# Preparation, fill and end of a patch-attention and DCT kernel laid out anew, with the first turn behind tile ten

## The reference, cut to what matters

```python
def _L0_conv_ref(x, W1, b1, a1, W2, b2, a2, Wa, ba, aa, Wd, bd):
    embed_w = prelu(conv1x1(x, Wa, ba), aa)
    match_in = prelu(conv1x1(x, W1, b1), a1)
    raw_w = extract_patches(embed_w, 6, 2)
    ref = x.reshape(B, C, H // 2, 2, W // 2, 2).mean(axis=(3, 5))
    ref = prelu(conv1x1(ref, W2, b2), a2)
    w = extract_patches(ref, 3, 1)
    wn = (w / norm(w)).reshape(B, -1, C // 2 * 9)
    xp = extract_patches(match_in, 3, 1).reshape(B, -1, C // 2 * 9)
    yi = softmax(einsum('blc,bqc->blq', wn, xp) * 10, axis=1)
    yd = conv_stride_2(transposed_conv(yi, raw_w), Wd) + bd
    return yd / 6

x = x + _L0_conv_ref(_gn(x), ...)
x = x + dct2(_gn(x))
```

## Time and profile before

| | us |
|---|---|
| median of 3 runs | 232.2 |
| lowest and highest | 231.97 and 234.13 |
| the profiled execution's own time | 232.2 |
| its span from first to last instruction | 230.4 |
| PE busy | 182.9 (79%) |
| DVE busy | 142.3 (62%) |
| ACT busy | 118.1 (51%) |
| POOL busy | 122.4 (53%) |

### The profile page before, as it was taken

One profiled execution on the slowest core, in us unless ns is written; L12 is line 12 of the kernel. 1 busy time (PEld: TensorE's weight loads), 2 busy tenths in 40 slices (PEclk: granted clock), 3 DMA queues, 4 the chain that ended last, 5 costly groups with the idle time before them and its releaser, 6 DMA issues.

```text
span 230.4 us, 3498 instructions
## 1 busy us (share of the span) xinstructions
PE 182.9 (79%) x1112; PEld 147.9 (64%) x1112; DVE 142.3 (62%) x293; ACT 118.1 (51%) x209; POOL 122.4 (53%) x107
## 2 busy tenths in 40 slices
PE   1496606963797589396999999999998999698993
PEld 0444506942666478185888878987876776577790
DVE  5669815663576767867566666556778379577101
ACT  4875612657373467545575695565564356133020
POOL 8362101006478489488686599999999940000000
PEclk9996555899679659979999999999999999997687
DMA  5270076666140000243542511440064000004402
GB/s 155 46 129 10 9 138 102 104 116 181 44 77 0 4 0 1 34 81 68 114 126 82 123 32 30 80 81 4 4 127 125 3 3 1 0 0 83 75 3 51
DMA packets 16872, 14.09 MB, mean 61 GB/s; under 512 B 9974, under 2 KB 14646, under 8 KB 16726
## 3 DMA queue, kind: packets, MB, share of 16 engines
q1 hardware_dynamic: 15174, 12.83, 27.7%
q10 hardware_dynamic: 1680, 1.04, 1.6%
HBM read 2.14 MB, written 1.18 MB: 14 GB/s over the span
## 4 chain that ended last, share of the span: by engine, by line
PE 50%; DVE 20%; ACT 9%; POOL 8%; issue 7%; ACTq 3%; DMA 1%; DVEq 0%; SPq 0%; POOLq 0%
PE yt L915 12%; PE ps L873 11%; PE zt L899 9%; POOL nt L692 4%; DVE negm L1392 4%; ACT nt L1105 3%; ACTq L365 3%; PE zt L935 2%; DVE mimg L1338 2%; DVE mhi L1334 2%; PE ps L899 2%; PE yt L950 2%; PE zt L873 2%; ACT slanted L1067 2%; PE pm L943 2%
## 5 line engine op out<-in xcount | busy, mean ns | idle before, releaser
L692 POOL TENSOR_TENSOR nt<-nt 128x599 f32<-128x599 f32 (+1 forms) x51 | 69.2, 1357 | 31.7 <-ACT nt L1113 24.0
L915 PE MATMUL yt<-yf,kf 125*128 125x384 f32 (+1 forms) x120 | 49.6, 497 | 4.8 <-DVE yf L1409 4.7
L899 PEld LDWEIGHTS zt<-ident,nt 128*125 128x125 f32 (+1 forms) x300 | 40.2, 181 | 12.7 <-issue 2.5
L899 PE MATMUL zt<-ident,nt 128*125 128x128 f32 (+1 forms) x300 | 42.4, 279 | 0.1
L1113 ACT ACTIVATE nt<-nt,rps 128x599 f32<-128x599 f32 x36 | 28.7, 796 | 20.0 <-DVE rps L1399 19.9
L1105 ACT ACTIVATE nt<-ps,negm 128x576 f32<-128x576 f32 x31 | 22.9, 738 | 30.3 <-DVE negm L1392 30.3
L1392 DVE TENSOR_REDUCE negm<-ps 128x1 f32<-128x576 f32 x31 | 23.4, 754 | 16.3 <-PE ps L873 15.8
L873 PE MATMUL ps<-wh,vh 128*128 128x288 f32 x62 | 18.5, 383 | 17.6 <-DVE wr L1387 9.1
L873 PEld LDWEIGHTS ps<-wh,vh 128*128 128x128 f32 x62 | 10.7, 214 | 24.1 <-ACT nt L1105 13.8
L915 PEld LDWEIGHTS yt<-yf,kf 125*128 125x128 f32 (+1 forms) x120 | 18.8, 192 | 5.9 <-DVE yf L1409 5.1
L1409 DVE COPY yf<-zt 125x384 f32<-125x384 f32 (+1 forms) x28 | 19.4, 691 | 4.2 <-issue 3.0
...
...
## 6 DMA issues: line engine op xcount, KB each, us to landing
...
vh<-mimg SPq DMA_DIRECT2D x24, 72.0 KB, 2.5
vl<-mimg SPq DMA_DIRECT2D x24, 72.0 KB, 2.5
...
```

The costliest lines, as they stand in the source:

```text
L692: pool.tensor_tensor(nt[:, dst, (to + 1) * KP + 1:(to + 1) * KP + 1 + n], nt[:, one, (row1 + 1) * KP + 1:(row1 + 1) * KP + 1 + n], nt[:, o ...
L899: last = nc.tensor.matmul(turned(sums_bank(m), n, column), keys_at(tile, r + dr, n, shift), ident[:, :], start=at == 0, stop=at == len(wor ...
L915: nc.tensor.matmul(yt[:, k % 2, 0:CHUNK], kf[b][0:n, blk, :], yf[0:n, blk, :], start=blk == 0, stop=blk == KB - 1).then_inc(s_mb, 1)
```

## The change

It has five parts.

1. `BEGIN` and with it `FILL` go from 11 to 10. Turn 0 comes one tile earlier in the order, so that turn `k` starts in the order behind tile `3k + 11` in place of `3k + 12`; there are 46 steps in place of 47.
2. The queries of image 0 for chunks 1 to 5 are loaded together: 16 DMAs of 16 partitions by five chunks in place of 30 (and three of `vr` in place of 15). Tiles of chunks 1 to 5 wait for all of them (`arrived`). `vr` is now loaded after the keys on ACT, and the first tile waits for its four operands one by one.
3. The tables `BEFORE`, `SPREAD` and `BEHIND_PE` are new. The row jobs of image 1 come one in each step from step 2 on, and DVE does a row's maximum a step after ACT has made its `slanted`. The keys of image 1 come from step 15 on in place of 13; the copies after the eighth row are a job of their own.
4. The memset of the odd taps on POOL is replaced by two DMAs at the start. The bias addition on ACT covers one column of 48 pixels; the rest of the bias is added in `join_taps`, which is now two instructions for each part in place of one. The last sums (`last_sum`) start one step earlier.
5. In the list `behind` 5 `idle` matmuls stand in place of 14, and the last transforms of the two images are interleaved.

```diff
-BEGIN = 11
+BEGIN = 10
-    ("conv1", 0, (7,)), ("match", 0, (6, 7)), ("ninth", 0, (0, 1, 2)), ("inorm", 0, (0, 1)), ("keys", 0, (0, 1)),
-    ("mean", 1, (0,))]
+    ("conv1", 0, (7,)), ("match", 0, (6, 7)), ("inorm", 0, (0, 1)), ("mean", 1, (0,)), ("dup", 0, (0,)), ("keys", 0, (0, 1)),
+    ("after", 0, (0,)), ("ninth", 0, (0, 1)), ("weights", 1, (0,))]
...
-    ("conv1", 1, 8, 9, 3.5), ("match", 1, 8, 11, 3.5),
+    ("emb", 0, 2, 4, 1), ("conv1", 1, 8, 7, 3), ("match", 1, 8, 7, 3), ("squares", 1, 1, 9, 1), ("dup", 1, 1, 29, 1),
...
-    "act": {"conv2": 1, "conv1": 1, "emb": 1, "ek": 1, "zn": 1, "d1": 1, "match": 2},
+    "act": {"conv2": 1, "conv1": 1, "emb": 1, "ek": 1, "match": 7, "after": 5},
...
+    "dve": {"bias_2": 1, "bias_1": 1, "bias_a": 3, "conv2": 3, "conv1": 3, "emb": 3, "norm": 2, "inorm": 2, "keys": 2,
+            "match": 4, "dup": 4},
...
-    behind = stages(1, ("deviation", 1)) + stages(0, ("zn", 3), ("d1", 2))
-    behind += stages(1, ("x1n", 3)) + stages(0, ("d2", 2)) + [("idle", 1, 8)] + stages(1, ("zn", 3)) + [("idle", 1, 4)]
-    behind += stages(1, ("d1", 2)) + [("idle", 1, 2)] + stages(1, ("d2", 2))
+    behind = stages(1, ("deviation", 1)) + stages(0, ("zn", 3)) + [("idle", 1, 3)] + stages(0, ("d1", 2))
+    behind += stages(1, ("x1n", 3)) + [("d2", 0, 0)] + stages(1, ("zn", 3)) + [("d2", 0, 1), ("idle", 1, 2)]
+    behind += stages(1, ("d1", 2), ("d2", 2))
...
+        def arrived(eng, landed, g, images):
+
+            together = 16 * (3 if landed is s_vr else sum(n for _, n in SHIFTS))
+            if images == 1:
+                eng.wait_ge(landed[min(g, 1)], together if g else 48)
+            else:
+                eng.wait_ge(landed[g], (96, together + 48, 48)[min(g, 2)])
...
+                            for row in range(n):
+                                to = F(dst[3 * CR * k + row:3 * CR * k + row + 1, cols])
+                                wide = dst.shape[1]
+                                to = bass.AP(to.tensor, to.offset, [[n * wide, CR], [1, CHUNK * many]])
+                                sp.dma_start(to, bass.AP(src.tensor, at + BLOCK * row,
+                                                         [[pitch, CR], [BLOCK, many], [1, CHUNK]])).then_inc(done, 16)
...
+            sp.wait_ge(s_zero, 3)
+            for b in range(B):
+                odd = v2[2 * C * b + C:2 * C * (b + 1), :]
+                sp.dma_start(odd, F(vr[128 - C:128, :])).then_inc(s_apart[b], 16)
             ref_patches(0)
-            for t in range(NCH):
-                match_patches(0, t)
+            match_patches(0, 0)
+            match_patches(0, 1, NCH - 1)
...
-                pool.memset(v2[2 * C * b + C:2 * C * (b + 1), :], 0.0).then_inc(s_apart[b], 1)
...
-                part = x1_rows(b)
-                nc.scalar.activation(v2[part, :], v2[part, :], ACT.Identity, bias=bd6[part, 0:1]).then_inc(s_xres[b], 1)
+                first = strided(x1(b), 0, (W, H))
+                nc.scalar.activation(first, first, ACT.Identity, bias=bd6[x1_rows(b), 0:1]).then_inc(s_xres[b], 1)
...
-                nc.vector.tensor_tensor(even, even, odd, ALU.add).then_inc(s_x1[b], 1)
-                dve.wait_ge(s_x1[b], part + 1)
+                for n in range(2):
...
+                    nc.vector.scalar_tensor_tensor(out=even, in0=even, scalar=bd6[x1_rows(b), 0:1], in1=odd, op0=ALU.add,
+                                                   op1=ALU.add).then_inc(s_x1[b], 1)
+                    dve.wait_ge(s_x1[b], 2 * part + n + 1)
```

More of the change, by code:

```diff
@@ L360, in strided, with ninth @@
             return bass.AP(ap.tensor, ap.offset + start, [list(ap.ap[0])] + [list(d) for d in dims])
[L362 to L366 removed]
+        def ninth(eng, n, low, t, many=1):
+            src = F(mimg[64 + low:64 + low + CR, :])
+            at = src.offset + match_rows_at(1 + SHIFTS[2][0], t + 2, 0)
+            return eng.dma_start(F(vr[CR * n:CR * (n + 1), CHUNK * t:CHUNK * (t + many)]),
+                                 bass.AP(src.tensor, at, [[mimg.shape[1], CR], [BLOCK, many], [1, CHUNK]]))
+        def arrived(eng, landed, g, images):
[4 more added lines that the diff above has]
+                eng.wait_ge(landed[g], (96, together + 48, 48)[min(g, 2)])
         def patches_in(eng, images):
[L370 to L372 removed]
+            for g in range(NCH if images > 1 else 2):
+                for landed in (s_vh, s_vl, s_vr):
+                    arrived(eng, landed, g, images)
         def place_free(eng):
@@ L578, in _ @@
                     row_before(b)
-                sp.wait_ge(s_x1[b], 3)
+                sp.wait_ge(s_x1[b], 6)
                 sp.dma_start(x1_copy[b], x1(b)).then_inc(s_x1out[b], 16)
@@ L1026, in match_high @@
                         after(b, 1)
-                        after(b, 2)
                     return
@@ L1531, in _ @@
                     sums_copied(k, KB - 1)
+                if k == NG - 3 and j == 1:
+                    last_pair(NG - 2)
+                if k == NG - 3 and j == 2:
+                    last_sum(0)
+                if k == NG - 2 and j < 2:
+                    last_sum(j + 1)
+                if k == NG - 2 and j == 2:
+                    last_pair(NG - 1)
                 if k >= 1 and j == 2 and (k - 1) % NCH in (2, 4, 5):
@@ L1537, in _ @@
                         x1_statistics(b, 2 * part + 1)
-                if k == NG - 3 and j == 1:
-                    last_pair(NG - 2)
-                if k == NG - 2:
-                    last_sum(j)
-                if k == NG - 2 and j == 2:
-                    last_pair(NG - 1)
                 perform(gaps["dve"].get((s, 2), []), handlers)
```

81 lines of the change are left out of this document (39 added, 42 removed).

## The result

| | before | after | forecast |
|---|---|---|---|
| median | 232.69 (4 runs) | 242.96 (4 runs) | 220.0 |
| lowest and highest | 231.97, 234.13 | 242.68, 243.86 | range 211 to 228.5 |
| span of the profiled execution | 230.4 | 240.9 | 218.2 |

The changed kernel is slower: the ratio is 1.044, with a 95% interval of 1.039 to 1.050. The time lies far outside the range, on the other side.

The account below looks back on a forecast made before the run. PE was taken to bound the middle, POOL right behind it in later turns, and engines waiting in a ring the fill. 5.5 - 10.6 - 3.7 + 0.3 + 0 - 3.7 = -12.2 from 232.2 gives 220.0 us; range 211 to 228.5.

Parts of the forecast that it names:

- Start to tile 3: Start to tile 3's end: waiting for merged loads at 115 GB/s covers tile 0's 4 us gain; +5.5 us.
- Tile 3 to turn 0: Fill up to the tile ahead of turn 0: eight shorter tile steps in place of nine; -10.6 us.
- one more tile lies in it, 1.1 us of PE: Turn 4 to turn 9: the earlier start adds one tile there, costing 1.1 us of PE.
- Turns 0 to 3: Turns 0 to 3: fewer rows and long jobs, 47.0 us in place of 50.73; -3.7 us.
- slower rival: Fill: every high part and split waits for a whole POOL sum, turns win nothing; 235.0 us, chance 0.06.
- I price that wait at 1.2: Turns 2 and 3: keys come just ahead of the tile needing them; PE's wait costs 1.2 us.
- Turn 4 to turn 9: Turn 4 to turn 9: one more tile, against a bias addition and a memset that leave; +0.3 us.
- The seven pairs of `join_taps` cost some 0.1 us each beside other work: Tap joins on DVE: each of seven two-instruction pairs costs some 0.1 us beside other work.
- The end: Behind the last turn: image 1's transposes start at 214.0 in place of 217.74; -3.7 us.
- faster rival: Load up to tile 3: the 16 DMAs run at their issue pace, +5.5 becomes 0; 214.5 us, chance 0.20.

Follow-up runs that it names:

- chunk_loads: Changed kernel with SyncE's match-patch loads chunk by chunk again, with a wait for each chunk; 237.3 us, ratio 1.016 to the kernel before.
- before_keys_first: Kernel before with image 0's keys ahead of ScalarE's nine DMAs of the third part, nothing else; 230.9 us, ratio 0.991.
- begin_eleven: Changed kernel with the first turn eleven tile steps behind the first tile, as before the change; 244.2 us, ratio 1.039 to the kernel before.
- chunks_late_eleven: Changed kernel with loads, joins, bias, end list and image 1's late jobs as before, and the first turn eleven steps behind; 227.6 us, ratio 0.980.
- near_later: Changed kernel with two VectorE copies of image 1's doubled rows and columns moved behind the next maximum; 244.8 us, ratio 1.049 to the kernel before.
- keys_early: Changed kernel with image 1's scaled and split keys moved earlier in the table (36 and 39 for 42 and 45); 242.0 us, ratio 1.031.
- chunks_and_keys: Changed kernel with SyncE's loads chunk by chunk and image 1's keys two steps earlier; 233.9 us, ratio 0.998 to the kernel before.
- before_two_joins: Kernel before with only the changed tap joining: two instructions for a pair, and ScalarE's bias addition for the first columns only; 235.7 us, ratio 1.012.
- one_join: Changed kernel with one addition for a join and ScalarE's bias over the whole image, both images' in turn 0; 245.3 us, ratio 1.041.
- one_join_split: Changed kernel with one addition for a join, whole-image ScalarE bias, and image 1's bias back in turn 4; 243.0 us, ratio 1.042.
- chunks_late_tables: Changed kernel, start still ten steps behind, with loads, joins, bias, end list and image 1's late jobs as before; 230.1 us, ratio 0.990.
- eleven_idle_end: As chunks_late_eleven, with the changed order of work behind the last turn but 16 idle jobs in place of 5; 222.6 us, ratio 0.949.

## Why the prediction was wrong

**Start to tile 3** (+5.5, it was +8.2). The mechanism was right, tile 3 waited for the DMAs; the size was off because I took 115 GB/s from three half microseconds, though my own stage row has 102, and over the whole load the merged ones reach 91 (the small ones of chunk_loads 87). The last two passes then ran at half clock, 1.3 us in place of 0.9. The step also counted tile 0's 4 us as won and then covered; before_keys_first shows that they are worth 0.9% of the time (0.4 to 1.4).

**Tile 3 to turn 0** (-10.6, it was -11.9). Right in the sum, partly by luck: the first two steps took 1.9 and 3.0 us where I had 4.0 each, the next five 3.8 on average where I had 3.4. And it was to be read against the load: at tile 12 the two effects have cancelled, 82.1 in both kernels.

**One turn earlier.** The step "one more tile lies in it, 1.1 us of PE" was wrong. It took a whole step from the fill, 3.4 us at the forecast's own pace, and put it back as the bare matmuls of a tile. A step of turns 4 to 8 took 49.45 / 15 = 3.3 us before the change already, because every step brings a third of a turn with it. What ends the kernel is tile 35 and POOL's sums behind it:

```profile
191.80 1.45 POOL L450 TENSOR_TENSOR nt<-nt 128x600 f32<-128x600 f32 x1
193.29 0.92 PE L918 MATMUL zt<-ident,nt 128*125 128x128 f32 x6 [3.18 <-POOL nt L450]
```

From tile 35's start to turn 9 it is 193.29 - 182.75 = 10.5 us, and 182.32 - 172.11 = 10.2 before. The distance of the turns does not enter, and neither begin_eleven nor chunks_late_eleven is slower for a distance of eleven. This step alone hid some 2 us of the miss, and it hid it in the term that looked like a gain.

**Turns 0 to 3** (-3.7, it was +4.7). Turn 0 was to take 14.5 us since a row and two long jobs left, and took 17.8; what stayed was DVE's chain beside POOL. I had counted the row's instructions at their undisturbed time and left out the two copies behind the eighth row, which only my slower rival names. This is read from the trace; near_later did not shorten the turn. Turns 2 and 3 took 26.6 in place of 21.7. For tile 18 I priced the wait for the keys at 1.2 us. The wait itself is 1.81 + 0.94, the late exponential stands behind the split of 1.43, and the clock falls behind it; together it is 5 to 6 us (keys_early, chunks_and_keys). "I price that wait at 1.2" is the step that failed: behind the wait comes the clock.

**Turn 4 to turn 9** (+0.3, it was +9.9). "The seven pairs of `join_taps` cost some 0.1 us each beside other work" failed (and there are six pairs, the 12 records above). They stand ahead of the maximum in DVE's step and cost 1.2 to 2.1 us more than one addition of 0.93, three times beside tiles. By tiles the 9.9 us are, rounded: 3.0 for the one step more, which I had priced at 1.1; 3.0 because the step ahead of tile 24, with turn 3's pair, takes 6.1; 3.5 from tile 24 to 35; 0.3 behind tile 35, for all that PE waits 3.18 us for POOL's late pair there. before_two_joins took 5.1 us more from tile 24 to 35, with the ACT additions gone in it; taken out of the changed kernel the pairs give back 2.1 to 3.9. That is the largest part that is shown. Some 2 us stay with one addition too (tile 28 to 32 takes 16.2 to 16.4 us in after, one_join and one_join_split, 14.3 before). With image 1's late jobs, the loads and the end as before as well it takes 13.3 (chunks_late_tables); which of these it is stays open.

**The end** (-3.7, it was -0.5). The order did what I said: image 1's transposes start 7.0 us behind the last turn. But I costed `idle` matmuls as time that is only lost, and took the durations behind them as they were with them. With five jobs of them image 1's first transform takes 5.35 us in place of 2.92. With sixteen, in nearly the same order, the gain is there: 4.2 us in eleven_idle_end against chunks_late_eleven.

**The rivals.** Neither slower nor faster rival came out as worked out. The slower one had the right lock (DVE beside POOL), but put it at full price into every step of the fill, where a step took 3.4 us on average and not 4.9; it bit in turn 0 and in the joins. The chance of 0.06 for slower was too small for a change with five parts, when the keys (1.2 us) and the joins (0.1) had only the price of the best case.
